# Folded attention: the first output product of the batch before, moved between the two tiles' scores

## The chip, the cores and the metric

One core of a Trainium2 chip runs the whole program. Its engines are TensorE (PE; PEld is its weight load), VectorE (DVE), ScalarE (ACT), GpSimd (POOL) and SyncE (SP, which issues DMAs). Each has its own in-order queue and waits for others by semaphores. The metric is device time in microseconds; the kernel before takes 968.2 us, the median of 3 runs (967.32 to 969.09).

## What is computed

x is 32 batches of 256 tokens by 256. A gated cross-attention over a context of 77 rows of 192 (8 heads of 64) is added to x, then a gated mixture of experts (16 experts, 2 chosen, and a shared one):

```python
x = x + tanh(g_xattn) * xattn(layernorm(x), ctx, Wq, Wk, Wv, Wout, bout)
x = x + tanh(g_ffn)   * moe(layernorm(x), Wg, W1, W2, Ws1, Ws2)
# xattn: softmax(q k^T / 8) v over 8 heads, then @ Wout + bout
```

Only the attention stage is touched here; it ends about half way through the span.

## The kernel before

Float32 accuracy is reached by splitting each operand into a high and a low half and multiplying three pairs of halves (`products`, L75 to 82: the matmuls appear at L79, L80 and L81).

Attention is folded: a group of 4 batches has its context multiplied into the query weights, which gives a matrix M (per head 77 columns, 616 in all), so that the scores of a batch are x times M; and the values are multiplied into the output weights, which gives a matrix VW of 616 rows by 256, so that the output is probabilities times VW. A batch has two tiles of 128 tokens, i = 0 and 1.

`attend` writes one loop per engine by hand, over groups g and batches q of a group (b = 4g + q). In a batch TensorE's queue has, in this order: `scores(b, 0)` (12 matmuls into the PSUM tile ps_s), two projection units for M of a later group (`make_M_units`), two parts of a later VW (`project_part`), `scores(b, 1)` into the same ps_s, `attend_out(b - 1, 0)` (15 matmuls into half of ps_o), `values`, two more projection units, the transposes of tile 0's probabilities, `attend_out(b - 1, 1)`, another part, `make_K`, the transposes of tile 1 and the rest of both. The last group (batches 28 to 31) has no projections, and from batch 28 on there are no parts either.

What these wait for:

- `scores(b, i)` waits until VectorE has read the tile before out of ps_s: its subtraction of the row maximum (L1074), which follows the maximum (L1071).
- `attend_out(b, 0)` waits for all transposed probabilities of b (PT_lo), for the low half of VW of b (`vw_lo`, L788), and for the residual (L1090) that last read its half of ps_o.

VectorE's queue in a batch: maximum and subtraction of tile 0, low halves of M, sums and reciprocal of tile 0 (L1081, L1084), maximum and subtraction of tile 1, `residual(b - 1, 0)`, sums and reciprocal of tile 1, low halves of values and M, and then the low halves of the probabilities, `residual(b - 1, 1)` and the low half of the keys.

GpSimd's queue in a batch: `norm(b, 0)` (probabilities times reciprocal, L778), the low half of the next batch's x (L270), some small work on statistics, `norm(b, 1)` (L778 again), the bias addition to x (L819, after its load), and `split_vw(b)`: the high half of VW (L786), then the low half (L788), after VW has been loaded.

VW takes a way through memory: TensorE makes it in parts, ScalarE copies them out of PSUM (L1007, behind its exponential of tile 0, L968), SP stores them (L704) and, behind the stores of a batch, loads the VW of batch b in two DMAs (`load_vw`, L717 and L719).

The lines around the change, at the middle of TensorE's batch:

```python
if b > 0:
    scores(b, g, q, 1)
if b > 0:
    attend_out(b - 1, 0)
```

Of the kernel before, what the change touches and what calls it, by code (L numbers as in the profile page):

```python
# [63 lines left out]
def wait(eng, sem, value):  # L64

    if not isinstance(value, int) or value > 0:
        eng.wait_ge(sem, value)
# [7 lines left out]
def products(nc, out, pairs, start=True, stop=True):  # L75

    last = None
    for n, (lh, ll, rh, rl) in enumerate(pairs):
        nc.tensor.matmul(out, lh, rh, start=start and n == 0, stop=False)  # L79
        nc.tensor.matmul(out, lh, rl, start=False, stop=False)  # L80
        last = nc.tensor.matmul(out, ll, rh, start=False, stop=stop and n == len(pairs) - 1)  # L81
    return last
# [227 lines left out]
def make_K(nc, pe, c, a, n):  # L310
    wait(pe, a.M_lo, 4 * n)
    keys(nc, c, a, a.ps_proj[1][:, 0:GK], n)
# [266 lines left out]
def attend(nc, c, a):  # L579


    with ExitStack() as ctx:
# [45 lines left out]
        def M_at(s, parity, cc, q, lo, size):  # L628

            return M[s][:, bass.ds(parity * MPAR + (cc * GB + q) * HK + lo, size)]  # L630
# [9 lines left out]
        def made_in(b):  # L640

            return b + AHEAD if 0 <= b and b + AHEAD < UNITS else None
# [44 lines left out]
        with nc.Block(no_gpsimd_drain=True) as block:  # L687
# [146 lines left out]
            def _(pe):  # L834
                def scores(b, g, q, i):
                    wait(pe, sub_done, 2 * b + i)
                    xs = xT[q % 2]
                    for half in range(2):
                        last = products(nc, ps_s[:, half, 0:HALF], [
                            (xs[0][:, k, i * P:(i + 1) * P], xs[1][:, k, i * P:(i + 1) * P],  # L840
                             M_at(0, g % 2, k, q, half * HALF, HALF), M_at(1, g % 2, k, q, half * HALF, HALF))
                            for k in range(DC)])
                    last.then_inc(score_done, 1)

                def values(n):

                    if n >= AHEAD:
                        part_is_copied(pe, n - 1, 1)
                    wait(pe, vT_lo, 2 * n - 2)
                    of_context(nc, c.wv_hi, c.wv_lo, context(a, n // GB), value_bank(n), n % GB, vT_done)  # L850

                def project_part(n, m):

                    lo, hi = PARTS[m]
                    pe.wait_ge(vT_lo, 2 * n + 2)
                    if 3 * n + m <= 3 * GB:
                        if 3 * n + m > 1:
                            part_is_copied(pe, n, m - 2)
                    elif m == 1:
                        part_is_copied(pe, n, 0)  # L860
                    elif m == 2:
                        wait(pe, PT_lo, 3 * (n - AHEAD) + 2)
                    bank, v = part_bank(n, m), values_set(n)
                    for j in range(2):
                        h, out = 2 * (n % GB) + j, bank[0:hi - lo, j, :]
                        nc.tensor.matmul(out, v[j][:, lo:hi], c.wo_hi[:, h, :], start=True, stop=False)
                        last = nc.tensor.matmul(out, v[j][:, lo:hi], c.wo_lo[:, h, :],
                                                start=False, stop=True)
                    last.then_inc(part_done, 1)

                def attend_out(b, i):

                    if i == 0:
                        pe.wait_ge(PT_lo, 3 * b + 3)
                        pe.wait_ge(vw_lo, b + 1)
                    wait(pe, x1_done, 2 * b + i)
                    hi, lo = VW[b % 2]
                    tokens = slice(i * P, (i + 1) * P)
                    rows = [P] * (CHUNKS - 1) + [LAST_ROWS]
                    products(nc, ps_o[:, i, :], [  # L880
                        (PT[0][0:r, k, tokens], PT[1][0:r, k, tokens], hi[0:r, k, :], lo[0:r, k, :])
                        for k, r in enumerate(rows)]).then_inc(out_done, 1)

                def transpose_probs(b, i):
                    pe.wait_ge(normed, 2 * b + i + 1)
                    wait(pe, PT_lo, 3 * b)
                    if i == 1 and (made_in(b - 1) or b == 0):
                        part_is_copied(pe, b - 1 + AHEAD, 2)
                    for k in range(CHUNKS - 1):
                        last = nc.tensor.transpose(ps_pt[i][:, k * P:(k + 1) * P], prob[i][:, k * P:(k + 1) * P],  # L890
                                                   c.ident[:, :])
                    last.then_inc(PT_done, 1)

                def transpose_rest(b):
                    pe.wait_ge(PT_lo, 3 * b + 1)
                    for i in range(2):
                        last = nc.tensor.transpose(rest_bank[:, i * P:(i + 1) * P], prob[i][:, (CHUNKS - 1) * P:HK],
                                                   c.ident[:, :])
                    last.then_inc(PT_done, 1)

                def make_M_units(b, q, head):

                    for k in (2 * head, 2 * head + 1):
                        make_M(nc, pe, c, a, b + GB, q, k)

                def body(g, first, last):
                    for q in range(GB):
                        b = GB * g + q
                        n = made_in(b)
                        pe.wait_ge(a.x_split, b + 1)  # L910
                        if q == 0:
                            pe.wait_ge(a.M_lo, 2 * H * (g + 1))
                        if b > 0:
                            scores(b, g, q, 0)
                        if not last:
                            make_M_units(b, q, 0)
                        if made_in(b - 1) or b == 0:
                            project_part(b - 1 + AHEAD, 1)
                            project_part(b - 1 + AHEAD, 2)
                        if b > 0:  # L920
                            scores(b, g, q, 1)
                        if b > 0:
                            attend_out(b - 1, 0)
                        if n:
                            if q == GB - 1:
                                pe.wait_ge(a.ctx_split, g + 3)
                            values(n)
                        if not last:
                            make_M_units(b, q, 1)
                        transpose_probs(b, 0)  # L930
                        if b > 0:
                            attend_out(b - 1, 1)
                        if n:
                            project_part(n, 0)
                            make_K(nc, pe, c, a, n)
                        transpose_probs(b, 1)
                        transpose_rest(b)
# [7 lines left out]
                for n in range(AHEAD):  # L945
                    if 0 < n < AHEAD - 1:
                        values(n + 1)
                    for m in range(1 if n == AHEAD - 1 else 3):
                        project_part(n, m)
                groups(body)  # L950
                busy(nc, c, ps_proj[1], c.bias[:, :], 5)
                for i in range(2):
# [1037 lines left out]
```

## Time and profile before

| | |
|---|---|
| median of 3 runs | 968.2 us (967.32 to 969.09) |
| profiled execution | 962.98 us |
| its span | 961.1 us |
| TensorE, VectorE, GpSimd busy, share of the span | 91%, 80%, 64% |
| granted TensorE clock, mean | 0.959 |
| last output product of attention begins | 478.62 us |

A profile is one execution. "Busy" counts the time of an engine's instructions; matmuls are pipelined, so that one of 0.28 us is followed by the next after 0.12 us. In a timeline each row has the start, the length, the engine, the line, the operation and, in brackets, the idle time before it and what ended it.

### The profile page before, as it was taken

The numbers are of one execution on the slowest core, as the hardware profiler recorded it, in microseconds if no ns is written. First come the engines' busy times: TensorE is split into PE (matmuls) and PEld (weight loads), VectorE is DVE, ScalarE is ACT, GpSimd is POOL, SyncE is SP. The second block draws the span as 40 slices with busy tenths as digits, with TensorE's granted clock in tenths as the row PEclk, the third lists the DMA queues.
The fourth block names the chain that finished last, engine by engine and source line by source line (L and its number), as shares of the span: only waits on it lengthen the run. The fifth ranks groups of instructions, "written<-read, shape, count | busy, mean of one in ns | idle before, by whom it ended". The sixth has DMA issues, their size and how long they took to land. (4 is left out here: it accounts for less than half of the span.)

```text
span 961.1 us, 20484 instructions
## 1 busy us (share of the span) xinstructions
PE 870.1 (91%) x6332; PEld 812.5 (85%) x6332; DVE 764.3 (80%) x1851; ACT 521.5 (54%) x1188; POOL 610.6 (64%) x623
## 2 busy tenths in 40 slices
PE   6658999999999999987779999999689999999996
PEld 6558999999999999977658888888569999699995
DVE  7637999999999999987558888888747788378885
ACT  6437878777878777643155555554124444144442
POOL 3424778888787878777743555555516677446676
PEclk9678999999999999999979999999889999999998
DMA  8045566666665666786362444443278999478892
GB/s 238 16 148 165 176 189 186 186 180 198 189 203 177 191 185 201 241 247 219 127 201 83 166 169 162 169 169 117 99 240 304 345 335 353 142 252 264 269 293 68
DMA packets 140756, 188.96 MB, mean 197 GB/s; under 512 B 14822, under 2 KB 104810, under 8 KB 140656
## 3 DMA queue, kind: packets, MB, share of 16 engines
q1 hardware_dynamic: 125296, 145.45, 49.5%
q0 software_dynamic: 15360, 42.24, 11.4%
q8 instruction: 56, 0.92, 0.4%
q14 instruction: 44, 0.36, 0.1%
HBM read 107.86 MB, written 86.09 MB: 202 GB/s over the span
## 5 line engine op out<-in xcount | busy, mean ns | idle before, releaser
L1319 POOL DMA_INDIRECT rows_scratch<-row,slot x64 | 67.9, 1061 | 74.9 <-DVE row L1572 60.3
L778 POOL TENSOR_TENSOR prob<-prob,row_sum 128x616 f32<-128x616 f32 x64 | 77.9, 1217 | 51.3 <-DVE row_sum L1084 49.6
L1725 POOL DMA_INDIRECT rows_scratch<-prow x80 | 78.7, 984 | 49.9 <-issue 46.4
L1725 POOL DMA_INDIRECT out<-prow x80 | 78.7, 984 | 49.6 <-issue 28.0
L79 PE MATMUL ps_s<-M_hi,xT_hi 128*128 128x308 f32 x256 | 84.8, 331 | 23.2 <-DVE prob L1074 15.5
L1835 ACT ACTIVATE eyT_hi<-ps_ey 128x512 fp32r<-128x512 f32 x80 | 47.9, 598 | 91.3 <-PE ps_ey L1747 90.6
L79 PE MATMUL ps_h<-w_flat,eyT_hi 128*128 x320 | 97.1, 304 | 0.0
L968 ACT ACTIVATE prob<-prob,rstd 128x616 f32<-128x616 f32 x64 | 52.0, 812 | 72.8 <-DVE prob L1074 72.8
L80 PE MATMUL ps_o<-VW_lo,PT_hi 128*128 128x256 f32 (+1 forms) x320 | 90.9, 284 | 0.0
L80 PE MATMUL ps_h<-w_flat,eyT_hi 128*128 x320 | 90.4, 282 | 0.0
L81 PE MATMUL ps_h<-w_flat,eyT_lo 128*128 x320 | 90.3, 282 | 0.0
L1879 DVE TENSOR_TENSOR eyT_lo<-ps_ey,eyT_hi 128x512 fp32r<-128x512 f32 x80 | 55.3, 692 | 32.2 <-ACT eyT_hi L1835 29.0
L80 PE MATMUL ps_s<-M_lo,xT_hi 128*128 128x308 f32 x256 | 78.7, 308 | 0.0
L81 PE MATMUL ps_s<-M_hi,xT_lo 128*128 128x308 f32 x256 | 78.7, 307 | 0.0
L79 PEld LDWEIGHTS ps_s<-M_hi,xT_hi 128*128 128x128 f32 x256 | 49.1, 192 | 30.7 <-DVE prob L1074 22.6
L1899 DVE SCALAR_TENSOR_TENSOR prow<-ps_z,prow 128x256 f32<-128x256 f32 x160 | 69.4, 475 | 0.5 <-PE ps_z L81 0.5
L1840 ACT ACTIVATE silu<-ps_h 128x256 f32<-128x256 f32 x80 | 30.7, 383 | 67.9 <-PE ps_h L81 67.9
L1888 DVE TENSOR_TENSOR a<-ps_h,silu 128x256 f32<-128x256 f32 x80 | 34.0, 425 | 36.7 <-ACT silu L1840 36.7
L80 PEld LDWEIGHTS ps_h<-w_flat,eyT_hi 128*128 128x128 f32 x320 | 61.8, 193 | 0.0
L80 PEld LDWEIGHTS ps_o<-VW_lo,PT_hi 128*128 128x128 f32 (+1 forms) x320 | 61.6, 192 | 0.0
L79 PEld LDWEIGHTS ps_h<-w_flat,eyT_hi 128*128 128x128 f32 x320 | 61.5, 192 | 0.0
L81 PEld LDWEIGHTS ps_h<-w_flat,eyT_lo 128*128 128x128 f32 x320 | 61.3, 192 | 0.0
(344 smaller groups left out, 3374.2 us busy)
## 6 DMA issues: line engine op xcount, KB each, us to landing
prow<-rows_scratch SPq DMA_DIRECT2D x160, 258.0 KB, 3.3
vw_raw<-vw_scratch SPq DMA_DIRECT2D x32, 512.0 KB
vw_scratch<-stage SPq DMA_DIRECT2D x60, 154.0 KB
rows_scratch<-blank SPq DMA_DIRECT2D x34, 258.0 KB, 3.8
xT_raw<-in_xT SPq DMA_DIRECT2D x32, 256.0 KB, 4.0
x_tok<-in_x SPq DMA_DIRECT2D x32, 256.0 KB, 4.9
x_scratch<-x_tok SPq DMA_DIRECT2D x32, 256.0 KB, 2.9
row<-x_scratch SPq DMA_DIRECT2D x16, 512.0 KB, 3.9
```

Of the source, the lines that this page charges most:

```text
L79: nc.tensor.matmul(out, lh, rh, start=start and n == 0, stop=False)
L80: nc.tensor.matmul(out, lh, rl, start=False, stop=False)
L81: last = nc.tensor.matmul(out, ll, rh, start=False, stop=stop and n == len(pairs) - 1)
L778: nc.gpsimd.tensor_tensor(pr, pr, row_sum[i][:, :].unsqueeze(2).broadcast_to((P, H, CK)), ALU.mult).then_inc(normed, 1)
L968: nc.scalar.activation(prob[i][:, :], prob[i][:, :], ACT.Exp, scale=c.rstd1[:, bass.ds(2 * b + i, 1)]).then_inc(exp_done, 1)
L1319: pool.indirect_dma_start(c.rows1, bass.IndirectOffsetOnAxis(slot1[:, t:t + 1], 0), row[G % NX][:, i, :], None).then_inc(scattered[G % NX] ...
L1725: pool.indirect_dma_start(dram, bass.IndirectOffsetOnAxis(target, 0), row[u][:, i, 0:columns], None, bounds_check=bound, oob_is_err=False) ...
L1835: nc.scalar.activation(yT[p][0][:, :, :], ps_y[p][:, :, :], ACT.Copy).then_inc(yT_hi, 1)
L1840: nc.scalar.activation(silu[p][:, :, :], ps_h[p][:, :, HID:], ACT.Silu).then_inc(silu_done, 1)
L1879: V.tensor_tensor(yT[p][1][:, :, :], ps_y[p][:, :, :], f32(yT[p][0][:, :, :]), ALU.subtract).then_inc(yT_lo, 1)
L1888: V.tensor_tensor(a[p][:, :, :], ps_h[p][:, :, 0:HID], silu[p][:, :, :], ALU.mult).then_inc(a_done, 1)
L1899: last = V.scalar_tensor_tensor(row[b][:, i, 0:D], ps_z[p][:, i, :], row[b][:, i, weight:weight + 1], row[b][:, i, 0:D], ALU.mult, ALU.add)
```

## The change

The output product of tile 0 of the batch before is issued ahead of `scores(b, 1)`, where it stood behind it. Nothing else changes: the same instructions, with the same waits.

```diff
                             project_part(b - 1 + AHEAD, 1)
                             project_part(b - 1 + AHEAD, 2)
                         if b > 0:
+                            attend_out(b - 1, 0)
                             scores(b, g, q, 1)
-                        if b > 0:
-                            attend_out(b - 1, 0)
                         if n:
                             if q == GB - 1:
                                 pe.wait_ge(a.ctx_split, g + 3)
```

## Rows read from the trace of the kernel before

**Rows 1.** Table by stretch (us, then busy time of each engine, PE's granted clock, DMA):
```profile
200.00:300.00 100.00, 97.73 (x741) 94.98 (x741) 92.00 (x181) 79.55 (x201) 80.44 (x83) 1.00 0.63 189
```

**Rows 2.** Waits of PE, 60 to 470 us (total, times, longest):
```profile
PE ps_s L79 <- DVE prob L1074: 15.5, 31, 1.7
```

**Rows 3.** Timeline of PE, first matmul of a block (start, length, what, idle before):
```profile
246.12 0.39 PE L79 MATMUL ps_s<-M_hi,xT_hi 128*128 128x308 f32 x1
...
248.47 0.28 PE L866 MATMUL ps_v<-wo_hi,vT 128*103 128x256 f32 x1
...
249.89 0.41 PE L79 MATMUL ps_s<-M_hi,xT_hi 128*128 128x308 f32 x1 [0.32 <-DVE prob L1074]
...
251.67 0.28 PE L79 MATMUL ps_o<-early,PT_hi 128*128 128x256 f32 x1
...
253.47 0.30 PE L79 MATMUL ps_v<-ctxM_hi,wv_hi 128*128 128x308 f32 x1
...
258.91 0.39 PE L79 MATMUL ps_s<-M_hi,xT_hi 128*128 128x308 f32 x1
```

**Rows 4.** Timeline of POOL, same stretch:
```profile
248.30 2.95 POOL L788 TENSOR_TENSOR VW_lo<-vw_raw,early 128x1280 fp32r<-128x1280 f32 x1
...
255.70 1.22 POOL L778 TENSOR_TENSOR prob<-prob,row_sum 128x616 f32<-128x616 f32 x1 [0.35 <-DVE row_sum L1084]
...
258.11 1.28 POOL L819 TENSOR_TENSOR x_tok<-x_tok,bias 128x512 f32<-128x512 f32 x1 [1.20 <-DMA x_tok<-in_x]
...
259.86 1.25 POOL L786 CAST VW_hi<-vw_raw 128x1280 fp32r<-128x1280 f32 x1 [0.47 <-DMA vw_raw<-vw_scratch]
...
261.20 2.96 POOL L788 TENSOR_TENSOR VW_lo<-vw_raw,VW_hi 128x1280 fp32r<-128x1280 f32 x1
```

**Rows 5.** Timeline of DVE, same stretch:
```profile
247.27 1.02 DVE L239 TENSOR_TENSOR PT_lo<-ps_pt,PT_hi 128x512 fp32r<-128x512 f32 x2
...
249.03 0.80 DVE L1074 TENSOR_TENSOR prob<-ps_s,row_max 128x616 f32<-128x616 f32 x1
...
251.87 0.80 DVE L1071 TENSOR_REDUCE row_max<-ps_s 128x8 f32<-128x616 f32 x1
...
253.74 0.42 DVE L1090 TENSOR_TENSOR x_tok<-ps_o,x_tok 128x256 f32<-128x256 f32 x1 [0.23 <-PE ps_o L81]
...
255.35 0.20 DVE L1084 RECIPROCAL row_sum<-row_sum 128x8 f32<-128x8 f32 x1
...
261.82 0.80 DVE L1074 TENSOR_TENSOR prob<-ps_s,row_max 128x616 f32<-128x616 f32 x1
```

**Rows 6.** Timeline of SP's queue: the second load of batch 14's raw product:
```profile
254.64 0.53 SPq L719 DMA_DIRECT2D vw_raw<-vw_scratch  x1
```

**Rows 7.** Timeline of POOL, last batches of attention:
```profile
434.86 1.22 POOL L778 TENSOR_TENSOR prob<-prob,row_sum 128x616 f32<-128x616 f32 x1 [1.70 <-DVE row_sum L1084]
...
438.59 2.90 POOL L788 TENSOR_TENSOR VW_lo<-vw_raw,VW_hi 128x1280 fp32r<-128x1280 f32 x1
...
446.20 1.22 POOL L778 TENSOR_TENSOR prob<-prob,row_sum 128x616 f32<-128x616 f32 x1 [1.35 <-DVE row_sum L1084]
...
472.59 2.88 POOL L788 TENSOR_TENSOR VW_lo<-vw_raw,early 128x1280 fp32r<-128x1280 f32 x1
```

**Rows 8.** Timeline of PE, last batches of attention:
```profile
440.45 0.41 PE L79 MATMUL ps_s<-M_hi,xT_hi 128*128 128x308 f32 x1 [1.72 <-DVE prob L1074]
...
475.57 0.36 PE L79 MATMUL ps_o<-early,PT_hi 128*128 128x256 f32 x1 [2.39 <-issue]
...
478.62 0.58 PE L79 MATMUL ps_o<-early,PT_hi 128*128 128x256 f32 x1 [0.59 <-DVE x_tok L1090]
...
481.77 0.41 PE L81 MATMUL ps_o<-early,PT_lo 104*128 104x256 f32 x1
```

**Rows 9.** Table by stretch, last batches and end of attention:
```profile
437.00:448.00 11.00, 8.49 (x64) 7.79 (x63) 8.37 (x15) 3.32 (x6) 8.67 (x7) 1.00 0.70 226
...
476.00:478.00 2.00, 2.00 (x14) 1.73 (x12) 0.00 (x0) 0.00 (x0) 1.57 (x6) 0.72 0.00 0
```

## The prediction

> **What bounds the kernel now.** I read the table by stretch first. Between 200 and 300 us, in the middle of attention, TensorE is busy 97.7 of 100 us at a granted clock of 1.00, VectorE 92 and GpSimd 80 [rows 1]: no engine has much room, and GpSimd's 80% matters below. The list of waits then says what the change aims at: the scores' first matmul waits for VectorE's subtraction 31 times, 15.5 us in all and at most 1.7 us at once [rows 2]: once in each batch after batch 0, 0.32 us in the batch shown below [rows 3], 1.72 us in the last ones [rows 8].
>
> The timeline of one batch (b = 14) gives the order. The period is 258.91 - 246.12 = 12.79 us. TensorE runs scores of tile 0 (246.12), a projection pair, two parts (248.47), waits 0.32 us, scores of tile 1 (249.89), the first output product of batch 13 (251.67), values (253.47) and so on [rows 3]. Each output product needs the value-weight product of its batch split in two halves by GpSimd. The reader should hold the low half of batch 13, ending at 248.30 + 2.95 = 251.25 [rows 4], against the output product at 251.67 [rows 3]: the product starts only 0.42 us after its last operand exists. In the next batch the low half ends at 264.16 and the product stands at 251.67 + 12.79 = 264.46: 0.30 us. So the product can't move ahead by more than that without a wait; the change moves it ahead of a block of 1.8 us plus the idle before it.
>
> **Part by part.** Nothing is added or removed: 15 matmuls (five row blocks, three products each; 251.67 to 253.47, 1.80 us) change places with 12 matmuls of scores. No DMA, and no instruction of another engine, is moved; TensorE alone has another order. What each wait of the moved block meets:
>
> - *The transposed probabilities.* Batch 13's low parts end at 247.27 + 1.02 = 248.29 [rows 5], before the parts of TensorE are through. Costs nothing.
> - *Its PSUM half*, freed by the residual of batch 12, one period earlier: nothing.
> - *The low half of the value-weight product*, 251.25. The two parts begin at 248.47 and hold 8 matmuls; at the output product's pace (1.80/15 = 0.12 us) they are issued by 249.43. So TensorE stops there 251.25 - 249.43 = 1.8 us in the first batch that meets it, longer than the 0.32 us that it loses now.
>
> Behind that wait now stand the scores of tile 1, the values, the second projection pair and both transposes, and for them wait VectorE (its maximum of tile 1 is ahead of everything else of the batch in its queue), ScalarE's second exponential, and GpSimd's second normalisation. And here is what makes the cost repeat: GpSimd works in order, and its next split stands behind that normalisation (L778) and the bias addition (L819). The change so closes a loop that was open: split, output product, scores, softmax, normalisation, next split. Its length, from one start of tile 1's scores to the next:
>
> - scores to maximum: 251.87 - 249.89 = 1.98 [rows 3, 5]
> - maximum to the end of the reciprocal: 255.55 - 251.87 = 3.68, less 0.19, because the residual waits 0.23 us for the output product now and would follow the subtraction after some 0.04: 3.49 [rows 5]
> - to the normalisation 0.15, normalisation 1.22, bias 1.28, high half 1.25, gap 0.09, low half 2.95: 6.94 [rows 4]
> - to TensorE 0.10, as between 472.59 + 2.88 = 475.47 and 475.57, where the product waited for just this [rows 7, 8]
> - the output product 1.80.
>
> Sum 14.31 us, no wait for memory in it. A second way around goes through the load: SP's issue of the raw product hangs, over ScalarE's copies of the parts, on the end of tile 0's subtraction (249.83), and lands 259.86 - 254.64 = 5.2 us after its issue, so that the low half ends 264.16 - 249.83 = 14.33 us after that subtraction [rows 4 to 6]. Then 0.10, product 1.80, scores to maximum 1.98, and from that maximum to the next batch's subtraction 262.62 - 251.87 = 10.75, less 0.19 [rows 5]: 28.77 us for two batches, 14.39 for one. The two differ by little; I take 14.33. That is 14.33 - 12.79 = 1.54 us more per batch, for the 28 batches 1 to 28: **+43.1 us**. (The first two, in which the loop closes, differ by tenths.)
>
> *The last batches* have no projections or parts, so TensorE waits 1.72 us for VectorE (440.45 [rows 8]), and the moved product would fit. But the low half of batch 28 ends at 438.59 + 2.90 = 441.49, after that wait is over. From normalisation to normalisation the period is 446.20 - 434.86 = 11.34 us. With the change: 441.49 - 434.86 = 6.63 to the split [rows 7], then 0.10 + 1.80 + 1.98 + 3.49 + 0.15: 14.15, or 2.81 more, three times: **+8.4 us**.
>
> *The clock there.* TensorE would stand idle nearly 3 us per batch between the scores of tile 0 and the product. The nearest row is the end of attention: after 2.39 us of idle the product starts at 475.57 [rows 8], and between 476 and 478 the mean granted clock is 0.72 [rows 9]; the next product runs at half clock and takes 478.62 to 482.18, 3.56 us in place of about 1.96 [rows 8]. Idles of 1.72 us leave the clock at 1.00 between 437 and 448 [rows 9]. If it falls likewise 1.3 us into the product, the product loses 0.5 us and the scores behind, 12 like matmuls, 1.3: 1.8 us in each of four batches. Bounds 0 and 7.2; one row can't say that it falls each time, so I take half, **+3.6**.
>
> The Trainium skill (TensorE: Matmul & The Clock Gate, Part 1) says that the half clock is the default and sustained activity releases it; that would have it fall in all four and give 7.2. The trace agrees in so far as the fall after 2.39 us shows it.
>
> Sum 43.1 + 8.4 + 3.6 = 55.1 us. The profiled execution took 962.98 us (span 961.1 and 1.9 around it), so 1018.1 by its own time; the median shown is 5.2 us above it, and 968.2 + 55.1 = 1023.3. Everything behind attention is shifted, not changed.
>
> A rule of the Trainium skill speaks for the change: Perfetto Trace Analysis, Optimization Strategies, asks to keep the matmul engine at high utilization. By it the 15.5 us of [rows 2] would be filled, and the time would be about 953. It is the first rival.
>
> **The rivals.** *Faster, by filling.* If the low half were there when the parts end, and tile 1's scores could come 1.3 us later without harm, the product would fill TensorE's waits: up to 15.5 us less, 953. It decides at a low half ending by 249.43 instead of 251.25. For it: TensorE is the busiest engine. Against it: those 0.42 and 0.30 us, and VectorE, which takes up tile 1's maximum at once as the scores end, so that any delay of them is its delay. 3 in 100.
>
> *Only the displacement.* If the splits kept ahead (a load that lands 1 us or more sooner once the period is longer, and a normalisation that lets the split through), the cost would be the displacement alone: scores of tile 1 start 249.43 + 1.80 = 251.23 instead of 249.89, 1.34 us later, less the 0.19 of the residual: 1.15 x 28 = 32.2, and nothing in the last batches: 1000. Against it: the loop of 14.31 holds no memory wait that could shrink. 8 in 100.
>
> *The clock falls more widely*, in the steady batches too, where TensorE's waits become longer, if scattered: at 1.8 us in one batch of three, 28/3 x 1.8 = 17 us beside all of the 7.2: about 1044. For it: the 2.39 us row. Against it: each single wait there is near 1 us or less in the steady state, and waits of 1.72 us left the clock at 1.00. 6 in 100.
>
> *No change* (the order is not felt): 1 in 100, 968.
>
> **How the numbers follow.** The forecast, the closed loop, has 82 in 100; its own range is 1011 (14.1 us per batch, no fall of the clock) to 1033 (14.5 and all falls). To leave out no more than 2 in 10, with room to both neighbours, I give 1004 to 1036. A measurement here can tell about 0.2%, 2 us. Faster 0.03, same 0.01, slower 0.96.
>
> **What would show it.** In the changed profile: the list of waits has the output product waiting for GpSimd's low half (L788) in nearly every batch, and VectorE's maximum waiting for the scores; the period in mid-attention is 14.2 to 14.5 us; TensorE's share falls from 97.7 to about 88 of 100, VectorE's from 92 to 82; the last three periods are 14 us or more, with a clock below 1.00 in some stretch. Attention ends 50 to 58 us later and all behind it keeps its length. I'm wrong if the period is below 14, if the product starts well after the low half's end, or if the last batches are not longer.

## The result, and the profile after

The changed kernel takes 1023.98 us (median of 4 runs, 1016.94 to 1027.59), the kernel before 968.64 us beside it (median of 4): a ratio of 1.0569, 95% interval 1.0521 to 1.0616. It is 5.7% slower. 1023.3 us was forecast.

The table by stretch of the changed kernel, in the columns of [rows 1]; the first line answers to that one, the others are the last batches:

```profile
200.00:300.00 100.00, 90.67 (x656) 84.61 (x655) 82.14 (x160) 69.13 (x177) 72.69 (x73) 1.00 0.57 169
...
484.00:498.00 14.00, 8.79 (x64) 8.14 (x64) 8.39 (x15) 3.40 (x7) 8.87 (x7) 1.00 0.54 175
498.00:513.00 15.00, 10.30 (x64) 9.64 (x64) 8.31 (x15) 2.45 (x5) 8.36 (x7) 0.89 0.42 141
513.00:530.00 17.00, 11.97 (x62) 10.95 (x62) 6.86 (x14) 2.97 (x5) 7.92 (x6) 0.80 0.31 103
```

Every engine works less per microsecond: VectorE 82 of 100 us instead of 92, GpSimd 73 instead of 80. No engine has become busier; a chain has become longer. In the last batches the granted clock falls, as the last column but two shows (0.89, 0.80; it was 1.00 there [rows 9]).

TensorE's waits between 60 and 535 us (total, times, longest):

```profile
PE ps_o L79 <- issue: 20.7, 29, 2.9
PE ps_v L866 <- DVE vT L239: 18.9, 27, 4.7
PE ps_o L79 <- DVE x_tok L1089: 17.0, 32, 1.6
```

The wait of the scores for VectorE, 15.5 us in [rows 2], is gone from the list: the change did what it says. The first line in its place is the moved product. "Issue" names no releaser; the timeline of batch 14 gives it. The other two lines are waits for VectorE, which the kernel before, between 60 and 470 us, has once (vT) or not at all (x_tok): VectorE now comes late for work further on in the batch, too. TensorE, first matmul of a block (answers to [rows 3]; `early` in a row is the buffer that holds the high half of VW of the odd batches, VW_hi that of the even ones):

```profile
251.56 0.39 PE L79 MATMUL ps_s<-M_hi,xT_hi 128*128 128x308 f32 x1
...
253.91 0.28 PE L866 MATMUL ps_v<-wo_hi,vT 128*103 128x256 f32 x1
...
255.22 0.35 PE L79 MATMUL ps_o<-VW_hi,PT_hi 128*128 128x256 f32 x1 [0.20 <-issue]
...
257.08 0.31 PE L79 MATMUL ps_s<-M_hi,xT_hi 128*128 128x308 f32 x1
...
265.89 0.39 PE L79 MATMUL ps_s<-M_hi,xT_hi 128*128 128x308 f32 x1
...
269.72 0.36 PE L79 MATMUL ps_o<-early,PT_hi 128*128 128x256 f32 x1 [0.39 <-issue]
```

GpSimd in the same stretch (answers to [rows 4]):

```profile
252.15 2.96 POOL L788 TENSOR_TENSOR VW_lo<-vw_raw,VW_hi 128x1280 fp32r<-128x1280 f32 x1
...
262.68 1.22 POOL L778 TENSOR_TENSOR prob<-prob,row_sum 128x616 f32<-128x616 f32 x1 [1.90 <-DVE row_sum L1083]
263.85 1.28 POOL L819 TENSOR_TENSOR x_tok<-x_tok,bias 128x512 f32<-128x512 f32 x1
...
265.33 1.26 POOL L786 CAST early<-vw_raw 128x1280 fp32r<-128x1280 f32 x1 [0.20 <-DMA vw_raw<-vw_scratch]
266.67 2.95 POOL L788 TENSOR_TENSOR VW_lo<-vw_raw,early 128x1280 fp32r<-128x1280 f32 x1
```

And VectorE's two maxima of that batch (answers to [rows 5]):

```profile
253.65 0.79 DVE L1070 TENSOR_REDUCE row_max<-ps_s 128x8 f32<-128x616 f32 x1
...
259.00 0.80 DVE L1070 TENSOR_REDUCE row_max<-ps_s 128x8 f32<-128x616 f32 x1 [1.81 <-PE ps_s L81]
```

The reader should see three ends meet. The low half ends at 252.15 + 2.96 = 255.11 and the product starts at 255.22; the next one ends at 269.62, and the product starts at 269.72: 0.11 and 0.10 us behind. So it is in each of the batches 2 to 31 (0.09 to 0.11 us). The scores of tile 1 start 1.86 us after the product, and VectorE stands 1.81 us before their maximum, which has no idle time before it in [rows 5] (25 such waits with 44.2 us between 60 and 430 us, 5 with 1.9 us in the kernel before). On GpSimd the normalisation, the bias and the split follow each other almost without a gap, where 1.20 and 0.47 us lay between them in [rows 4]. That is the loop of the prediction. The 0.20 us that are left before the high half are a wait for the load, the second way around: it shows in 6 of the 31 splits behind the first (0.20 to 0.43 us), so the two ways, 14.31 and 14.39 us, bind by turns. The period here is 265.89 - 251.56 = 14.33 us; from batch 1 to batch 27 its mean is 14.35.

Last batches, GpSimd's normalisation of tile 1 and low half (answers to [rows 7]), then TensorE's product and the scores behind it (answers to [rows 8]):

```profile
477.83 1.22 POOL L778 TENSOR_TENSOR prob<-prob,row_sum 128x616 f32<-128x616 f32 x1 [4.13 <-DVE row_sum L1083]
481.56 2.88 POOL L788 TENSOR_TENSOR VW_lo<-vw_raw,VW_hi 128x1280 fp32r<-128x1280 f32 x1
...
491.95 1.22 POOL L778 TENSOR_TENSOR prob<-prob,row_sum 128x616 f32<-128x616 f32 x1 [4.15 <-DVE row_sum L1083]
...
507.56 1.22 POOL L778 TENSOR_TENSOR prob<-prob,row_sum 128x616 f32<-128x616 f32 x1 [5.69 <-DVE row_sum L1083]
...
524.39 1.22 POOL L778 TENSOR_TENSOR prob<-prob,row_sum 128x616 f32<-128x616 f32 x1 [8.11 <-DVE row_sum L1083]
```

```profile
470.48 0.36 PE L79 MATMUL ps_o<-early,PT_hi 128*128 128x256 f32 x1 [2.95 <-issue]
...
484.54 0.36 PE L79 MATMUL ps_o<-VW_hi,PT_hi 128*128 128x256 f32 x1 [2.86 <-issue]
...
498.66 0.36 PE L79 MATMUL ps_o<-early,PT_hi 128*128 128x256 f32 x1 [2.89 <-issue]
...
514.27 0.55 PE L79 MATMUL ps_o<-VW_hi,PT_hi 128*128 128x256 f32 x1 [2.87 <-issue]
...
517.61 0.46 PE L79 MATMUL ps_s<-M_hi,xT_hi 128*128 128x308 f32 x1
...
531.08 0.36 PE L79 MATMUL ps_o<-early,PT_hi 128*128 128x256 f32 x1 [2.39 <-issue]
```

The periods are 14.12, 15.61 and 16.83 us, where they were 11.34, 11.35 and 11.32. The first of the three is the loop alone (14.15 forecast); in the other two the clock falls after a wait of 2.9 us. In the first of these it falls in the middle of the product; in the second the product at 514.27 runs at half clock from its start (granted clock 0.50; 3.34 us from it to the scores at 517.61 instead of 1.87), and so do the first of the scores.

The last product of attention begins 533.70 - 478.62 = 55.1 us later than before. Behind attention the profiled execution is longer by another 6 us, though nothing there is changed: from the first matmul after attention to the end it took 476.0 us in the profile before and 481.5 in this one, and between 476.1 and 481.9 in those of the seven kernels below; the 476.1 belong to one with the new order in every batch, so the order is not what makes it longer. That is spread of executions, and none of the verdicts below rests on it.

### The profile page after: what moved, and what is told of

Read it like the earlier page. It is cut to its first block and busy times, and to the rows that moved or that the text cites. A ratio compares the mean times of both kernels' runs of the same rounds, so it can differ in the third digit from the quotient of the medians.

```text
span 1022.1 us, 20484 instructions
## 1 busy us (share of the span) xinstructions
PE 888.2 (87%) x6332; PEld 817.7 (80%) x6332; DVE 765.4 (75%) x1851; ACT 516.3 (51%) x1188; POOL 609.2 (60%) x623
## 5 line engine op out<-in xcount | busy, mean ns | idle before, releaser
L1070 DVE TENSOR_REDUCE row_max<-ps_s 128x8 f32<-128x616 f32 x64 | 50.9, 796 | 71.4 <-PE ps_s L81 71.4
L79 PE MATMUL ps_s<-M_hi,xT_hi 128*128 128x308 f32 x256 | 82.7, 323 | 9.4 <-POOL xT_lo L270 9.3
L79 PE MATMUL ps_o<-early,PT_hi 128*128 128x256 f32 (+1 forms) x160 | 48.1, 301 | 21.0 <-issue 12.7
L79 PE MATMUL ps_o<-VW_hi,PT_hi 128*128 128x256 f32 (+1 forms) x160 | 48.7, 304 | 17.0 <-DVE x_tok L1089 8.7
```

The source lines that it names most:

```text
L1070: nc.vector.tensor_reduce(mx, S, AX.X, ALU.max).then_inc(max_done, 1)
```

## The experiments

My theory was the closed loop. The rivals were that the displacement of the scores by 1.8 us of work is everything, with the split only an accident beside it; that the wait for the split is everything; and, for the last batches, that the clock falls for another reason.

**The wait for the split taken away.** The product of tile 0 is given the output weights, which always lie in SBUF, in place of VW, so that part of the result is left out; the product of tile 1 takes over the wait.

```diff
 if i == 0:
     pe.wait_ge(PT_lo, 3 * b + 3)
+else:
     pe.wait_ge(vw_lo, b + 1)
 wait(pe, x1_done, 2 * b + i)
-hi, lo = VW[b % 2]
+hi, lo = VW[b % 2] if i else (c.wo_hi, c.wo_lo)
```

> New order, but the product of tile 0 multiplies the probabilities by the output weights that lie in SBUF all the time, not by VW (this part of the result is left out); the product of tile 1 then waits for the split. Closed loop (mine): with the wait for the low half gone, only the displacement is left: a period of about 13.9 us instead of 14.33 in mid-attention, and near 11.1 us in the last batches instead of 14 to 17; about 1000 us (995 to 1004). Rival, the displacement is everything and the split's wait incidental: period still 14.3, 1015 us or more. Rival, the wait for the split is everything: the product then fills the gap, period 12.8 or less, 968 or less.

Measured: 993.36 us, ratio to before 1.0265 (1.0218 to 1.0311), 1.6 us below the range that I gave. The mean period from batch 1 to 27 is 13.84 us; the last four periods are 11.2 us each. TensorE and VectorE in one batch:

```profile
246.88 0.39 PE L79 MATMUL ps_s<-M_hi,xT_hi 128*128 128x308 f32 x1
...
250.16 0.28 PE L79 MATMUL ps_o<-wo_hi,PT_hi 128*128 128x256 f32 x1
...
251.92 0.31 PE L79 MATMUL ps_s<-M_hi,xT_hi 128*128 128x308 f32 x1
...
255.94 0.35 PE L79 MATMUL ps_o<-VW_hi,PT_hi 128*128 128x256 f32 x1 [0.43 <-DVE x_tok L1090]
...
258.44 0.36 PE L866 MATMUL ps_v<-wo_hi,vT 128*103 128x256 f32 x1 [0.48 <-DVE vT L239]
...
259.34 0.41 PE L79 MATMUL ps_proj<-ctxM_hi,wk_hi 128*128 128x308 f32 x1 [0.18 <-DVE M_lo L239]
...
260.73 0.39 PE L79 MATMUL ps_s<-M_hi,xT_hi 128*128 128x308 f32 x1
```

```profile
253.83 0.80 DVE L1071 TENSOR_REDUCE row_max<-ps_s 128x8 f32<-128x616 f32 x1 [1.33 <-PE ps_s L81]
```

The product starts without a wait, and still VectorE stands 1.33 us before the maximum. It doesn't make up for that: TensorE then waits for it three times in the same batch (0.43, 0.48 and 0.18 us), where [rows 3] had one wait of 0.32 us, so the displacement too comes back in every batch. Both rivals are half right, and the runs give the shares. From the end of batch 1's first subtraction to that of batch 28, attention takes 343.95 us before, 372.23 here and 385.96 in the changed kernel: of the 42.0 us lost in these 27 periods, 28.3 are displacement and 13.7 what the wait for the split adds to it. (No run has the wait without the displacement in these batches.) In the last batches it is the wait alone: without it they are slightly shorter than before.

**Its control**, the same substitution in the old order:

> Control: the order of before with the same substitution (tile 0's product with the resident output weights, so no wait for the split; that part of the result is left out). All theories: within 3 us of before, 965 to 970, since the product did not wait for the split in the old order but in batch 28 (1.39 us).

Measured: 965.28 us, ratio 0.9981 (0.9952 to 1.0010); mean period 12.80 us against 12.79. The substitution itself moves nothing, so the comparison above holds.

**The new order in the last group alone**, the edit against the changed kernel:

```diff
-if b > 0:
+if b > 0 and last:
     attend_out(b - 1, 0)
     scores(b, g, q, 1)
+elif b > 0:
+    scores(b, g, q, 1)
+    attend_out(b - 1, 0)
```

> New order in the last group alone (batches 28 to 31), old order before it. Closed loop: there the scores of tile 1 wait for the low half, which comes 5.4 us after the normalisation: batch 28 some 3.4 us longer, the next three 14.15 us instead of 11.34, and 0 to 7 us for a falling clock: 980 to 988. Rival, displacement alone: VectorE's wait of 1.72 us is filled and the last batches are unchanged or up to 1 us shorter: 967 to 969.

Measured: 983.16 us, ratio 1.0175 (1.0125 to 1.0225). From batch 27's second normalisation on, the periods are 18.25, 14.10, 15.61 and 15.42 us, where before they were 12.90, 11.34, 11.35 and 11.32: 16.5 us more. In the changed kernel the same four periods lost 13.8 us, a quarter of its loss in attention. Batch 28 loses 5.35 us rather than 3.4: the product waits 5.07 us there, and the fall of the clock comes on top, as the table shows:

```profile
430.94 0.55 PE L79 MATMUL ps_o<-early,PT_hi 128*128 128x256 f32 x1 [5.07 <-issue]
```

```profile
420.00:440.00 20.00, 12.83 (x84) 12.18 (x83) 10.61 (x20) 5.38 (x10) 10.54 (x11) 0.83 0.61 182
440.00:460.00 20.00, 12.12 (x89) 11.00 (x87) 12.62 (x23) 4.95 (x10) 14.51 (x10) 1.00 0.60 191
460.00:480.00 20.00, 13.59 (x80) 12.95 (x81) 9.39 (x17) 3.72 (x6) 11.20 (x8) 0.83 0.47 155
```

**Both ways to the split shortened**, in the new order:

```diff
-load_x(sp, c, a, b, par)
 load_vw(b)
+load_x(sp, c, a, b, par)
...
+if b > 0:
+    split_vw(b)
 pool.wait_ge(a.x_in[par], 16 * (2 * g + q // 2 + 1))
 # (the bias addition to x)
-split_vw(b)
+if b == 0:
+    split_vw(b)
```

> New order, with both ways around shortened: SP loads VW ahead of x (0.76 us of issue sooner), and GpSimd splits VW ahead of the bias addition (1.28 us sooner). Closed loop: way by GpSimd 14.31 - 1.28 = 13.03, way by the load (28.77 - 0.8)/2 = 13.98, so the displacement's 13.9 to 14.0 us becomes the bound: 28 x 0.35 = 10 us less than the changed kernel, and up to 1.28 us less in each of the last three batches: 1008 to 1014. Rival, the split is not on the path and displacement sets 14.33: no gain, 1020 or more.

Measured: 1005.60 us, ratio 1.0401 (1.0352 to 1.0450). The mean period is 14.03 us (13.98 expected), the last three 12.91, 12.88 and 12.89 (14.15 - 1.28 = 12.87 expected). The time is 2.4 us below the range that I gave. The last three periods are 7.9 us shorter than in the changed kernel, and 4.2 of these are the fall of the clock that the changed kernel paid in its last two: the wait on TensorE, now at most 2.3 us, left the clock at 1.00. A new order in SP's and GpSimd's queues alone takes 0.3 us off TensorE's period, as summed: the loop does run through them. Which of the two edits did it, GpSimd's rows tell:

```profile
262.25 1.25 POOL L786 CAST early<-vw_raw 128x1280 fp32r<-128x1280 f32 x1 [1.15 <-DMA vw_raw<-vw_scratch]
```

In each of the batches 1 to 27 the split, now ahead of the bias, waits 0.6 to 1.2 us for its load. Of the two ways only the one by the load binds there, and the gain is the earlier load's; in the last four batches the split waits for no load, and the gain is the earlier split's.

**TensorE kept busy in the last group**, new order: `busy` issues ten matmuls whose result nobody reads.

```diff
+if last:
+    busy(nc, c, ps_proj[1], c.bias[:, :], 5)
 if b > 0:
     attend_out(b - 1, 0)
     scores(b, g, q, 1)
```

> New order, with 10 idle matmuls of 0.23 us each between the scores of tile 0 and the product in the last group, where TensorE waits 2.9 us. If the waits make the clock fall there: clock 1.00 to the end of the group, and the last three periods 14.1 us each instead of 14.12, 15.61 and 16.83: 4 us less than the changed kernel in attention, about 1019 to 1021. Rival, the clock falls for another reason: no change of those periods, 1023 to 1025.

Measured: 1017.78 us, ratio 1.0530 (1.0480 to 1.0581). The last three periods are 14.12, 14.12 and 14.09 us, and the clock stays:

```profile
484.00:498.00 14.00, 10.84 (x75) 9.84 (x74) 8.25 (x16) 3.49 (x6) 8.89 (x7) 1.00 0.55 176
498.00:513.00 15.00, 11.75 (x78) 10.29 (x76) 8.72 (x16) 3.50 (x6) 9.90 (x7) 1.00 0.48 155
513.00:527.00 14.00, 9.23 (x62) 8.22 (x62) 6.78 (x13) 2.45 (x5) 7.67 (x6) 1.00 0.37 121
```

So the idle time is what lowers the clock there, and its price in the changed kernel's profile is (15.61 - 14.12) + (16.83 - 14.09) = 4.2 us. The product's wait is 0.7 us here. The time itself came out below the 1019 to 1021 us that I expected; the times, 1017.8 against 1024.0, carry the spread behind attention, and the periods are the evidence.

**Only what is ready, ahead of the scores.** The high half of VW is there 3 us before the low one, and 10 of the 15 matmuls need only it. In the old order, `early` of these go ahead of the scores of tile 1, and the others, with the wait for the low half, behind them:

```diff
 if b > 0:
+    early = 10 if last else 4
+    out_early(b - 1, early)     # waits for PT_lo, vw_hi, x1_done
     scores(b, g, q, 1)
-if b > 0:
-    attend_out(b - 1, 0)
+    out_late(b - 1, early)      # waits for vw_lo
```

> Old order, but 4 of the 10 matmuls of tile 0's product that need only the high half of VW (ready 3 us before the low one) are issued ahead of the scores of tile 1, 10 of them in the last group; the rest stays behind the scores. 4 x 0.12 = 0.48 us fill TensorE's gap and delay no scores. If what hurts in the changed kernel is the low half's wait and the displacement of the scores, and not the place itself: nothing lost, the product ends 0.48 us sooner, VectorE's residual no longer waits 0.23 us: 27 x 0.19 + 4 x 0.2 = 6 us less than before, 961 to 964. Rival, VectorE is held elsewhere: same as before, 967 to 970. Rival, any piece ahead of the scores costs: above 971.

Measured: 962.76 us (median of 12 runs), ratio to before 0.9962 (0.9935 to 0.9989): faster than before by 0.4%, little, but the periods agree. The mean period is 12.67 us instead of 12.79, the last three are 11.20 instead of 11.34. One batch on TensorE, the last matmul ahead of the scores, the scores, and the first one behind them:

```profile
248.31 0.27 PE L895 MATMUL ps_o<-early,PT_lo 128*128 128x256 f32 x1
...
248.46 0.41 PE L79 MATMUL ps_s<-M_hi,xT_hi 128*128 128x308 f32 x1
...
250.27 0.28 PE L902 MATMUL ps_o<-early,PT_hi 128*128 128x256 f32 x1
```

and VectorE's residual, which no longer waits for TensorE (0.23 us in [rows 5]):

```profile
252.02 0.41 DVE L1112 TENSOR_TENSOR x_tok<-ps_o,x_tok 128x256 f32<-128x256 f32 x1
```

I expected 0.19 us per batch and got 0.12; VectorE is now busy 93 of 100 us in mid-attention. Batch 28 got longer, 13.90 us instead of 12.90: all ten go ahead there, and they wait for the high half:

```profile
424.62 0.36 PE L895 MATMUL ps_o<-early,PT_hi 128*128 128x256 f32 x1 [1.91 <-issue]
```

**All ten of them, in every batch:**

> As the one with 4, with all 10 matmuls that need only the high half ahead of the scores in every batch. No wait for the low half; displacement 10 x 0.12 - 0.5 = 0.7 us, less 0.19: +0.5 us in 27 batches, period 13.3, 980 to 984. Rival, only the wait for the low half costs: 961 to 968.

Measured: 978.02 us, ratio 1.0112 (1.0062 to 1.0161), 2 us below the range that I gave. The mean period is 13.27 us, VectorE waits 0.74 us on average before the maximum of tile 1, and the last periods are 11.2 us. With no wait for the low half in it, this is the displacement by itself, at another size: some 0.7 us of it (an estimate, ten matmuls of 0.12 us less a gap of 0.5) cost 0.48 us per batch, 13.27 - 12.79.

## Why the prediction was right

Point by point, by its own steps:

- *The wait for the low half.* Right: the product starts 0.10 us after it, as the step had it. The stop of 1.8 us in the first batch that meets it was not seen: TensorE stops 0.56 us in batch 2, and at most 0.5 us in the batches up to 27. Batch 1, whose product finds its operand ready, was already 13.98 us long.
- *The loop, 14.31 to 14.39 us.* Right: 14.35 on average. (Of two ways around, the longer should set the period; 14.33 between the two had no reason, and 0.06 us is too little to matter.) 43.1 us were forecast for 28 periods; the second normalisation of batch 28 ends 479.05 - 436.08 = 43.0 us later than before.
- *The last batches.* 8.4 us for the loop and 3.6 for the clock, 12.0 together; measured 12.55 from the normalisation of batch 28 to that of 31. The loop alone is right to 0.03 us (14.12 against 14.15). The clock fell in two of the four batches and cost 1.5 and 2.7 us, 4.2 together, where 1.8 each was reckoned. Half of 7.2 was a choice between bounds, not knowledge: in the run with the new order in the last group alone it fell in three of four.
- *The total.* That 1023.3 meets 1023.98 so closely is in part luck: the half taken for the clock, and executions that differ by 6 us behind attention alone. The lower end of the forecast's own range, 1011, comes out of its terms as 1013 (968.2 + 28 x 1.31 + 8.4).
- *The signs.* VectorE's share (82) and the end of attention came as said. TensorE is busy 90.7 of 100 us where about 88 was said, and what lies behind attention did not keep its length in this profile, by spread. The clock did not fall more widely: it is 1.00 from 85 to 498 us.
- *The displacement rival's price.* 1.15 us per batch forecast; the run without the wait gives 13.84 - 12.79 = 1.05. As a rival to the whole time it is refuted (993 against 1024).
- *What I would put otherwise.* The prediction tells the loss as the loop's. The loop sets the period, but two thirds of what the period lost, 28.3 of 42.0 us, would be lost without it, since VectorE has no slack for later scores. Each of the two is a loss by itself: the displacement in the run without the wait (993 us), the wait in the last batches, whose period without it is 11.2 us.
- *The rule on the busy matmul engine.* The Trainium skill, Perfetto Trace Analysis, Optimization Strategies, wants the matmul engine kept at work. The wait that it would fill was filled, and the time grew by 5.7%; the four ready matmuls in the same place fill it too and take 0.4% off. The same section of the Trainium skill goes on that it is the engines which block the critical path that are to be improved. The runs agree with that part: a load and a split that come sooner took 0.32 us off each period (14.35 to 14.03).
- *The rule on the clock.* The Trainium skill, TensorE: Matmul & The Clock Gate, Part 1, has the half clock as the default, which activity releases. The trace agrees in so far as idle time lowers the clock and work keeps it, with 0.89 and 0.80 in two stretches and 1.00 with the idle matmuls. That it falls after each such wait is what the prediction read into the rule to get 7.2 us, and it does not hold here: after waits of 2.95 and 2.86 us the clock stayed at 1.00.

## What to carry to other kernels

Before work is moved into an engine's gap, look up when its last operand is finished: a gap of 0.3 us tells nothing of work whose operand is ready 1.8 us later, and if that operand's maker waits, through other queues, for what now stands behind the moved work, the delay comes back in each round. Sum the loop from rows of the profile, around all engines and not on the busiest alone; here that gave the period to within 0.05 us. What may go into the gap is the piece that is ready and about as long as the gap: four matmuls of 0.12 us gained 0.4%, ten in every batch lost 1.1%.

## What the runs showed of the hardware

After TensorE waits of 2.9 us the clock fell in some batches and not in others of the same execution: not after those of 2.95 and 2.86 us at 470.48 and 484.54, but after the 2.89 us at 498.66. At the end of attention the same wait of 2.39 us was followed by a fall in the kernel before (0.72 between 476 and 478 [rows 9]) and by none in the changed one (product at 531.08; 1.00 between 531 and 535.8). The wait's length alone did not decide it.
